# A graph convolution in two float32r passes where three bfloat16 passes stood, with the 0/1 matrix expanded on chip

## The reference

```
def sage_conv(x, src, dst, Wl, bl, Wr):
    msg_sum = segment_sum(x[src], dst)          # sum of the neighbours' features
    agg = msg_sum / max(degree, 1)
    return agg @ Wl.T + bl + x @ Wr.T
h = relu(sage_conv(x, ..., W1l, b1l, W1r))
x = layernorm(x + sage_conv(h, ..., W2l, b2l, W2r))
```

## Time and profile before

| | |
|---|---|
| time, median of 3 runs | 5596.16 us (5591.11 to 5609.0) |
| the profiled execution: its own time | 5605.28 us |
| its span, first to last instruction | 5603.4 us |
| granted TensorE clock, mean | 0.89 |
| second SAGE convolution, line 930 on `h_pieces` | 892.1 to 1306.5 us |
| busy over the span: TensorE, VectorE, ScalarE, GpSimd | 79%, 47%, 57%, 57% |

### The profile page before, as it was taken

One profiled execution on the slowest core, in us unless ns is written; L12 is line 12 of the kernel. 1 busy time (PEld: TensorE's weight loads), 2 busy tenths in 40 slices (PEclk: granted clock), 3 DMA queues, 4 the chain that ended last, 5 costly groups with the idle time before them and its releaser, 6 DMA issues.

```text
span 5603.4 us, 86440 instructions
## 1 busy us (share of the span) xinstructions
PE 4453.9 (79%) x30196; PEld 3138.0 (56%) x30196; DVE 2632.7 (47%) x7852; ACT 3177.9 (57%) x4502; POOL 3190.0 (57%) x3114
## 2 busy tenths in 40 slices
PE   2688999996666666666566666599999979999998
PEld 1466666663344334434343434477777757777776
DVE  5888882113656666566666666212222221222222
ACT  2566661002444444444444444399888978888887
POOL 5000000004777777777777777477777746777775
PEclk7799999997777878788887888799999989999999
DMA  3223324654555656565555556567776766666664
GB/s 96 87 113 143 121 113 157 241 217 128 145 168 145 175 146 173 142 174 152 160 166 147 169 146 173 186 224 259 255 262 219 260 228 204 207 212 207 212 208 157
DMA packets 629486, 994.44 MB, mean 177 GB/s; under 512 B 359122, under 2 KB 511324, under 8 KB 625212
## 3 DMA queue, kind: packets, MB, share of 16 engines
q1 hardware_dynamic: 159412, 552.80, 27.7%
q0 software_dynamic: 146944, 302.80, 19.0%
q10 hardware_dynamic: 322696, 133.28, 8.8%
HBM read 715.99 MB, written 272.14 MB: 176 GB/s over the span
## 4 chain that ended last, share of the span: by engine, by line
PE 37%; POOL 23%; issue 8%; DVE 4%; DMA 3%; ACT 1%; SPq 1%; ACTq 0%; DVEq 0%; POOLq 0%
PE couple_bank L1530 27%; POOL messages L1481 23%; PE bank L1496 5%; DMA slices<-relations_d 1%; DMA messages<-table,src_rows 1%; PE bank L1568 1%; SPq L1401 1%; DVE ring L1839 1%; PE bank L1554 1%; DVE scaled L1832 1%; DVE type_scaled L1832 1%; DMA type_scaled<-node_hot 1%; PE bank L1544 1%; PE couple_bank L1512 1%; ACT lots L1318 0%
## 5 line engine op out<-in xcount | busy, mean ns | idle before, releaser
L1481 POOL DMA_INDIRECT messages<-table,src_rows x2320 | 2415.9, 1041 | 820.7 <-issue 652.9
L1318 ACT CAST lots<-slices 128x1024 fp32r<-128x1024 fp8e4 (+1 forms) x1750 | 1674.4, 1027 | 260.2 <-PE couple_bank L1530 216.1
L1530 PE MATMUL couple_bank<-lots,pieces 128*128 128x512 f32 x6860 | 1715.6, 403 | 16.5 <-ACT lots L1318 16.3
L1647 ACT CAST stage<-couple_bank 128x980 fp8e4<-128x980 f32 x896 | 841.0, 985 | 1132.1 <-PE couple_bank L1512 978.4
L1530 PEld LDWEIGHTS couple_bank<-lots,pieces 128*128 128x128 f32 x6860 | 1256.7, 189 | 325.9 <-ACT lots L1318 57.4
L1496 PE MATMUL bank<-group_hot,messages 128*128 128x120 bf16 x9084 | 692.4, 234 | 399.4 <-DMA messages<-table,src_rows 359.1
L1496 PEld LDWEIGHTS bank<-group_hot,messages 128*128 128x128 bf16 x9084 | 584.5, 107 | 662.6 <-issue 615.6
L1481 POOL DMA_INDIRECT messages<-table,rel_rows x708 | 688.7, 973 | 326.3 <-issue 173.6
L1793 DVE TENSOR_TENSOR ring<-ring,bank 128x120 f32 x354 | 99.1, 280 | 1464.8 <-PE bank L1496 1461.4
L1512 PE MATMUL couple_bank<-rel_hot,lo_dense_hot 128*128 128x490 bf16 x1792 | 597.6, 446 | 196.1 <-ACT stage L1647 178.3
L1462 POOL IOTA iota_rel_i<- 128x120 int32 (+1 forms) x4 | 1.7, 469 | 1185.7 <-DMA table<-typed_rows 1185.7
(11 more groups left out here) (272 smaller groups left out, 3851.2 us busy)
## 6 DMA issues: line engine op xcount, KB each, us to landing
slices<-relations_d SPq DMA_DIRECT2D x210, 768.0 KB
relations_d<-stage ACTq DMA_DIRECT2D x336, 240.0 KB
adjacency_d<-adjacency SPq DMA_DIRECT2D x15, 4704.0 KB, 14.5
adjacency<-adjacency_d SPq DMA_DIRECT2D x15, 4704.0 KB, 15.3
slices<-relations_d SPq DMA_DIRECT2D x70, 832.0 KB
pieces<-dense SPq DMA_DIRECT2D x42, 896.0 KB, 11.0
messages<-table,src_rows POOLq DMA_INDIRECT x2320
dense<-table_halves SPq DMA_DIRECT2D x49, 640.0 KB
```

The lines of the kernel that those rows point to most:

```text
L1318: return copy(to, of_slice[:, :, first:end, :])
L1481: pool.indirect_dma_start(messages_in(i)[:, t, 0:ROWS[v]], None, GATHERED[v], bass.IndirectOffsetOnAxis(ap=rows[:, e:e + 1], axis=0)).then ...
L1530: mm = pe.matmul(bank[DENSE_BANKS[K % 2]][:, 0:DENSE_COLS], pieces[M % PIECE_RING][:, tile % PIECE_TILES, half * P:(half + 1) * P], lots[l ...
L1647: act.copy(to, from_banks, saturate=False).then_inc(rel_evicted, 1)
```

## The change

Four things change.

`h` is kept as two float32r halves, `h_halves` (high, and the rest as a float32 difference), in place of three bfloat16 pieces. The first convolution's finish loses one ScalarE copy (1058) and one VectorE subtraction (1162 or 1165).

A task of the second convolution is 98 products (49 tiles x 2 halves) in place of 147, each with float32r weights (128 x 128) and a float32r moving operand.

The adjacency, stored as bfloat16, is widened to float32r on chip: `sage_lots` is a ring of three buffers of two tiles (128 x 768 float32r), filled from `adjacency` by ScalarE (lots of even number) and VectorE (odd), 25 lots a task, 13 by one engine and 12 by the other, in turn. A lot waits for the adjacency's load and for the last product on the lot three before it (`sage_lots_used`, or `chunk_summed` where that was a task's last lot). `SAGE_LOTS_AT` places lot `l` of a task at the tick after that product's tick, which is tick `l-2`, ahead of that tick's finish, in the lists of ScalarE and VectorE. TensorE waits for the lot ahead of the first of its four products.

`x1_T`, the copy of the stage's output, shrinks from the whole array to two chunks used in turn; its store counts on `typed_out` with the other store, and ScalarE waits for the stores of two tasks before.

The core of the diff; the rest renumbers semaphore counts and layout:

```diff
+SAGE_LOT_TILES = 2
+SAGE_LOT_RING = 3
+SAGE_TASK_LOTS = -(-NODE_TILES // SAGE_LOT_TILES)
...
-        (h_pieces,), _ = lay(X2, ("h_pieces", [P, NODE_TILES, PIECES, P], bf16))
+        (h_halves,), h_halves_end = lay(X2, ("h_halves", [P, NODE_TILES, HALVES, P], f32r))
...
+        SAGE_LOTS_AT = {}
+        for lot in range(CHUNKS * SAGE_TASK_LOTS):
+            at_tick = sage_lot_end(lot - SAGE_LOT_RING) + 1 if lot >= SAGE_LOT_RING else (CHUNKS + 1) * TICKS
+            SAGE_LOTS_AT.setdefault(divmod(at_tick, TICKS), []).append(lot)
...
+        def expand_sage(engine, copy, lot):
+
+            k, l = CHUNKS + lot // SAGE_TASK_LOTS, lot % SAGE_TASK_LOTS
+            c, first = TASKS[k][1], l * SAGE_LOT_TILES
+            end, cols = min(first + SAGE_LOT_TILES, NODE_TILES), chunk_tiles(TASKS[k][1]) * P
+            if stage_of(k):
+                engine.wait_ge(adjacency_in[HALF[c]], stage_of(k))
+            else:
+                engine.wait_ge(evicted, UNITS * 2)
+            if lot >= SAGE_LOT_RING:
+                task, of_task = divmod(lot - SAGE_LOT_RING, SAGE_TASK_LOTS)
+                if of_task == SAGE_TASK_LOTS - 1:
+                    engine.wait_ge(chunk_summed, CHUNKS + task + 1)
+                else:
+                    engine.wait_ge(sage_lots_used, task * (SAGE_TASK_LOTS - 1) + of_task + 1)
+            return copy(sage_lots[lot % SAGE_LOT_RING][:, 0:end - first, 0:cols], adjacency[HALF[c]][:, first:end, 0:cols])
...
-                    mm = pe.matmul(bank[SUM_BANKS[k % 2]][:, 0:cols], pieces[:, h, piece, :], adjacency[HALF[c]][:, h, 0:cols],
-                                   start=(m == 0), stop=(m == NODE_TILES * PIECES - 1))
...
+                        h, half = m // HALVES, m % HALVES
+                        lot = (k - CHUNKS) * SAGE_TASK_LOTS + h // SAGE_LOT_TILES
+                        if half == 0 and h % SAGE_LOT_TILES == 0:
+                            pe.wait_ge(*sage_lot_made(lot))
+                        if k == CHUNKS and half == 0 and h % CHUNK_TILES == 0:
+                            pe.wait_ge(low_made, h // CHUNK_TILES + 1)
+                        mm = pe.matmul(to, h_halves[:, h, half, :], sage_lots[lot % SAGE_LOT_RING][:, h % SAGE_LOT_TILES, 0:cols], start=(m == 0), stop=(m == STEPS[1] - 1))
+                        if half and (h + 1) % SAGE_LOT_TILES == 0:
+                            mm.then_inc(sage_lots_used, 1)
...
                     if tick == 8:
                         vec.wait_ge(high_made, k + 1)
-                        vec.wait_ge(middle_made, k)
-                        vec.tensor_tensor(by_tile(rest), by_tile(odd), pieces(0), ALU.subtract).then_inc(rest_made, 1)
-                    if tick == 10:
-                        vec.wait_ge(middle_made, k + 1)
-                        vec.tensor_tensor(pieces(2), by_tile(rest), pieces(1), ALU.subtract).then_inc(low_made, 1)
+                        vec.tensor_tensor(h_half(1), by_tile(odd), h_half(0).bitcast(f32), ALU.subtract).then_inc(low_made, 1)
...
             for s in range(SLOTS):
                 for u in range(TICKS + 2):
+                    for lot in SAGE_LOTS_AT.get((s, u), []):
+                        if lot % 2:
+                            expand_sage(vec, vec.tensor_copy, lot).then_inc(sage_lots_by_vec, 1)
```

More of the change, by code:

```diff
@@ L784, in resnorm_gnn, with sage_lot_end @@
         groups_before = lambda c: c * (TICKS // COUNT_UNITS)
-        STEPS = NODE_TILES * PIECES
+        STEPS = [NODE_TILES * PIECES, NODE_TILES * HALVES]
+        def sage_lot_end(lot):
+            k, l = CHUNKS + lot // SAGE_TASK_LOTS, lot % SAGE_TASK_LOTS
+            step = min((l + 1) * SAGE_LOT_TILES, NODE_TILES) * HALVES - 1
+            return (k + 1) * TICKS + max(u for u in range(TICKS) if STEPS[1] * u // TICKS <= step)
+        SAGE_LOTS_AT = {}
+        for lot in range(CHUNKS * SAGE_TASK_LOTS):
+            at_tick = sage_lot_end(lot - SAGE_LOT_RING) + 1 if lot >= SAGE_LOT_RING else (CHUNKS + 1) * TICKS
+            SAGE_LOTS_AT.setdefault(divmod(at_tick, TICKS), []).append(lot)
         BUILD_BANKS, SUM_BANKS, FIN_BANKS = (0, 1, 2, 3), (4, 5), (6, 7)
@@ L932, in dense @@
-                if last == NODE_TILES * PIECES:
+                    if m == 0 and k >= 2:
+                        pe.wait_ge(averaged, k - 1)
+                    to = bank[SUM_BANKS[k % 2]][:, 0:cols]
+                    if conv == 0:
+                        h, piece = m // PIECES, m % PIECES
+                        if m == 0:
+                            pe.wait_ge(evicted, (units_before(c) + units_of(c)) * 2)
+                        if k == 0 and m == 0:
+                            pe.wait_ge(x_split, X_SLICES)
+                            pe.wait_ge(x_middle, X_SLICES)
+                        mm = pe.matmul(to, x_pieces[:, h, piece, :], adjacency[HALF[c]][:, h, 0:cols], start=(m == 0), stop=(m == STEPS[0] - 1))
+                    else:
+                        h, half = m // HALVES, m % HALVES
[7 more added lines that the diff above has]
+                            mm.then_inc(sage_lots_used, 1)
@@ L933, in dense @@
+                if last == STEPS[conv]:
                     mm.then_inc(chunk_summed, 1)
@@ L1052, in finish @@
                             act.wait_ge(dense_codes_out, 32)
-                        act.copy(h_pieces[:, c * CHUNK_TILES:c * CHUNK_TILES + tiles, 0, :], odd[:, 0:cols].rearrange("p (t f) -> p t f", f=P)).then_inc(high_made, 1)
+                        act.copy(h_halves[:, c * CHUNK_TILES:c * CHUNK_TILES + tiles, 0, :], odd[:, 0:cols].rearrange("p (t f) -> p t f", f=P)).then_inc(high_made, 1)
                     if tick == 9:
@@ L1071, in finish @@
                         act.wait_ge(x1_back, seen + 1)
-                        act.copy(x1_T[:, c * CHUNK:c * CHUNK + cols], odd[:, 0:cols]).then_inc(x1_kept, 1)
+                        if seen >= 2:
+                            act.wait_ge(typed_out[n], 32 * (seen // 2))
+                        act.copy(x1_T[:, n, 0:cols], odd[:, 0:cols]).then_inc(x1_kept, 1)
                     if tick == 16:
-                        act.wait_ge(rest_made, X1_SPLITS + seen + 1)
+                        act.wait_ge(rest_made, X1_SPLITS - CHUNKS + seen + 1)
                         act.copy(rows[:, :, TYPE_WORDS + P:TYPE_WORDS + 2 * P], rest[:, 0:cols].rearrange("p (t f) -> p t f", f=P)).then_inc(middle_made, 1)
@@ L1078, in sage_scalar @@
                 for u in range(TICKS + 1):
+                    for lot in SAGE_LOTS_AT.get((s, u), []):
+                        if lot % 2 == 0:
+                            expand_sage(act, act.copy, lot).then_inc(lots_by_act, 1)
                     if (s, u) in SPANS_AT:
@@ L1305, in lots_made @@
         def lots_made(lot):
-            return lots_by_act, lot + 1
+            return lots_by_act, SAGE_LOTS_BY_ACT + lot + 1
         def expand(engine, copy, lot):
@@ L1373, in conv_sync @@
             sp.wait_ge(inverse_out, 32)
-            sp.wait_ge(x1_spilled, 16 * CHUNKS)
+            for n in range(2):
+                sp.wait_ge(typed_out[n], 32 * len(range(n, CHUNKS, 2)))
             sp.dma_start(lo_dense[:, :], lo_d).then_inc(dense_codes_in, 16)
@@ L1741, in conv_scalar @@
                 if v == 0:
-                    act.wait_ge(x1_spilled, 16 * CHUNKS)
+                    for n in range(2):
+                        act.wait_ge(typed_out[n], 32 * len(range(n, CHUNKS, 2)))
                 if v == 1:
```

80 lines of the change are left out of this document (36 added, 44 removed).

## The result

| | before | changed |
|---|---|---|
| median | 5599.93 us (5591.11 to 5609.0, 4 runs) | 5513.31 us (5506.47 to 5519.18, 4 runs) |
| ratio | | 0.9839, 95% interval 0.9827 to 0.985 |
| span of the profiled execution | 5603.4 us | 5517.3 us |
| granted TensorE clock | 0.89 | 0.886 |

Faster by 87 us where 90 were forecast (5506, range 5470 to 5546).

The account below looks back on a forecast made before the run. TensorE's products in the second convolution were taken as the bound, with the stage's end passed on. Terms -104.6 + 8 + 8 + 1 - 3 + 0.4 = -90 us gave 5506 us against the median of 5596.2, range 5470 to 5546.

Parts of the forecast that it names:

- TensorE is the bound, and the end of the stage is passed on: Second convolution: TensorE busy 100.00 of 100 us; each microsecond gained or lost moves the relational part's start one to one.
- A product: Second convolution: a float32r product of 384 columns takes 0.177 us, between 0.1626 and 0.179.
- Full tasks: Second convolution's 16 full tasks: 18.65 us each instead of 25.19, -104.6 us, plus 0.5 us a task for late lots.
- Where the lots cost: Walk through a task's ticks: TensorE waits for late lots or rows, 0.5 us a task, +8 in 16 tasks.
- Task 17: Second convolution's 128-column task: 98 products that can't hide a weight load, +8 us, between +2.9 and +14.1.
- Loads: Second convolution: adjacency loads hidden by 1.7 us, except once in slot 20 behind extra arrays, +1 us (0 to 4).
- First convolution: TensorE waits less for a one-hot behind the removed subtraction: -3 us in 16 slots (0 to -9).
- The store of `x1_d`: Stage end: the relational part also waits for this store, issued 0.42 us after the other, +0.4 us.
- The sum: Whole kernel: -104.6 + 8 + 8 + 1 - 3 + 0.4 = -90 us.
- two passes at 384 columns: Rival, second convolution: float32r costs 0.324 us a product like plain float32, tasks 33.1 us, kernel 5736 us; chance 0.05.
- lots in step: Rival, second convolution: TensorE waits at every lot, 40 us at copies of 1.5 us, kernel 5546 us; chance 0.09.
- the load bound: Rival, second convolution: loads 20% slower set the pace, +2.2 us a task, 35 us, kernel 5541 us; chance 0.06.

Follow-up runs that it names:

- all seven kernels: Changed kernel, two bfloat16 products, lots not refreshed, finish two ticks later, one-tile lots in a ring of six, both those edits, all lots by ScalarE; 5482.4 to 5540.0 us.
- the lots that are not refreshed: Changed kernel with only the first 28 lots widened, later products reading the buffers as they stand; 5498.0 us, ratio 0.9822 to the kernel before.
- The later finish: Changed kernel with the second convolution's finish two ticks later from the transposes on; 5499.9 us, ratio 0.9809 to the kernel before.
- the second executions: The kernel before and the changed kernel each run again unchanged; iota to first product on lots took 2279.5 and 2271.2 us.
- the kernel with two bfloat16 products: Kernel before without the low piece of h in the second convolution: 98 bfloat16 products a task, no lots; 5482.4 us, ratio 0.9796.

## Why the prediction was right, step by step

- **TensorE is the bound, and the end of the stage is passed on.** Shown: the relational part starts 95.5 us earlier, and where no copy and no load is late a task follows its products (17.23 us at 0.1626, 18.33 at 0.174). That the stage's end is passed on is borne out by all seven kernels: their last product is 96.1, 115.8, 102.7, 99.3, 99.9, 102.9 and 68.9 us earlier than before, in the order of the table, and their medians are 86.6, 119.0, 103.5, 107.0, 98.5, 116.8 and 66.9 us under that of the kernel before beside which each ran (5599.9 for the first, 5601.5 for the next two, 5606.9 for the others). The two differ by 14 us at most, on both sides, less than the scatter of 19 above.
- **A product.** Taken 0.177, bounds 0.1626 and 0.179; measured 0.1746 (median 0.173). The proportion, 0.175, would have been the better choice. The excess over the columns is 13 to 15 ns at 384, 19 at 512. 98 x 2.4 ns are 0.24 us a task, 3.8 in all. That it is the format's own, not the copies' traffic, was argued from line 1530 and is shown by the lots that are not refreshed.
- **Full tasks.** Taken 18.65 + 0.5; measured 18.97, and 18.33 without lots. The terms behind it were each off a little in opposite directions: products and finish 0.32 less, lots 0.64 in place of 0.5. From the first load to the last mean, 405.0 us became 307.2: -97.8 where -104.6 + 8 + 1 = -95.6 stood.
- **Where the lots cost.** The walk through the ticks gave 0.7 us of wait for `normed` where VectorE has the even ticks and none in the other parity. The parities are there, and the wait is 0.56 us by the difference of the tasks. The later finish shows that it is this wait. The 0.3 us for ScalarE's copies behind `normed` was not seen; the "up to 0.1" around a task's end is 0.26 to 0.36 (18.69 against 18.43 and 18.33) and is in both parities. So of the 0.64 us a task, 0.28 is the finish's wait in every second task and 0.36 the waits at the start of each.
- **Task 17.** This term was mis-sized: the middle between one column a clock and two float32 passes, +8. From TensorE's first product of the task to the load that follows its end it was 9.29 us and is 12.09, **+2.8**, the lower end. A float32r product of 128 columns takes 0.112 us, no more than a plain float32 product of 128 columns did, weights included (0.115); the second pass of the upper bound is not there. The Trainium skill (TensorE: Matmul & The Clock Gate, "LDWEIGHTS (loading the stationary operand)") gives 107 ns for a load of 128 columns, and the estimate from that is +2.1; the trace is near it. The 57 ns for a product before was 6.36 / 111 with the last one's own length left in; the products stand 56 ns apart.
- **Loads.** Hidden but once, +1, as taken. The first task behind the issue of slot 20's arrays is 21.89 us, but it holds other products of TensorE too, for which it was 2.8 us over the others before (27.97 against 25.19), and without them it is no longer than its parity's 19.25. The next is 19.75 us, 1.06 over its 18.69, and in it TensorE stands 0.85 us for a lot. The rival was close, though: tasks of 18.3 us were enough for it to cost 4.5, and of 17.2 for 9.
- **First convolution.** Taken -3; nothing. Task 17's first product is issued at 891.1 us against 892.2, and at 891.2 against 891.5 in the second executions; the kernel with two bfloat16 products, whose finish there is unchanged, has it at 890.8. A one-hot that came 0.3 us late once was not a gain per slot.
- **The store of `x1_d`.** +0.4 taken; the iota starts 11.3 us after the last mean in place of 10.7.
- **The sum.** Up to the relational part the terms give -90, the measurement -95.5: 5 for task 17, 2 for the tasks, 2 the other way in the first convolution. The whole time moved by 87, inside the scatter of what follows. That it came so near to 90 is luck in part: the terms were 5 us short, and the scatter of what follows took 9 of the 95.5 away.

The rivals: two passes at 384 columns is excluded by 0.1746; lots in step by the 18.33 without lots; the load bound only waits behind.

## What to carry to other kernels

A new product's price can be read from the nearest shape by its excess over the columns, and the time for a copy that hides behind it by room against duration; then walk the slot once for each parity. What cost here was a finish step that stands behind a copy in an engine's list, which running the steps behind it two ticks later took away, and a lot that came late at the start of each task, which lots of half the size in a ring of six took away. For an engine's capacity take the distance between neighbours in a run, not the duration of one. When a stage shrinks, look at what it covered: here the last small load landed about 17.8 us after the adjacency's issue, which left 7 us to spare in 25.2, 1 in 19, and none at 17.2, where it cost 9 us over the stage.

## What was not expected of the hardware

- Float32r products of 128 columns, each with its own weights, stand 0.112 us apart, where bfloat16 ones stand 0.056 apart and the columns are 53 ns. At 384 columns the excess is 13 to 15 ns, so it is not a slower stream of columns. That it is the load of the weights fits, but no run here tells it from another fixed cost.
- The excess of a float32r product over one column a clock is 19 ns at 512 columns and 13 to 15 at 384, and it hardly depends on what VectorE and ScalarE do in SBUF meanwhile (0.1737 against 0.1746 us).
- Copies of 768 elements on ScalarE last 0.835 us and start 0.735 apart.
